# The first ten steps of a four-layer graph network in an order of their own, written out engine by engine

## What is computed

```
h = relu(layernorm(x))                      # ahead of every layer
layer 0: Wh = h @ W0; e = leaky(Wh@a1 + (Wh@a2).T); p = softmax(where(adj > .5, e, -9e15), axis=1)
         x = x + elu(p @ Wh)
layer 1: Ah = adj + I; d = rsqrt(rowsum(Ah)); x = x + relu((d*Ah*d) @ h @ W1 + bias)
layer 2: x = x + relu(adj @ h @ W2) * rowmask(h)
layer 3: x = x + relu([h, adj @ h / deg] @ W3.T)
```

## Time and profile before

| | us |
|---|---|
| median of 3 runs (2557.01 to 2562.32) | 2560.43 |
| the profiled execution: its time, and its span in the trace | 2557.61, 2555.8 |
| PE busy | 2482.3 (97% of the span) |
| DVE busy | 2021.0 (79%) |
| ACT busy | 1397.8 (55%) |
| POOL busy | 1224.1 (48%) |
| chain that ended last: PE's share | 95% |

### The profile page before, as it was taken

The page is one execution under the profiler, slowest core; times in us unless marked ns, Lnnn a source line. Parts: engine busy times, 40 slices in busy tenths (PEclk is TensorE's granted clock), DMA queues, the critical chain, the costliest instruction groups (busy, mean ns, idle before and its releaser), DMA issues.

```text
span 2555.8 us, 40394 instructions
## 1 busy us (share of the span) xinstructions
PE 2482.3 (97%) x13094; PEld 2135.8 (84%) x13094; DVE 2021.0 (79%) x4373; ACT 1397.8 (55%) x2571; POOL 1224.1 (48%) x1607
## 2 busy tenths in 40 slices
PE   2799999999999999999999999999999999999998
PEld 2688888888888888888888888888888888888887
DVE  6788878888888888788888888888788878878853
ACT  3565555555555555555556555555555555555542
POOL 2545545544544544544544545445445455455431
PEclk8899999999999999999999999999999999999999
DMA  4112222222222222221221222222222222222210
GB/s 144 44 42 57 55 66 54 57 67 52 59 67 51 60 66 51 60 67 49 62 66 50 62 59 56 63 58 57 61 59 57 60 61 56 60 61 56 49 34 25
DMA packets 355889, 149.40 MB, mean 58 GB/s; under 512 B 279520, under 2 KB 320096, under 8 KB 355680
## 3 DMA queue, kind: packets, MB, share of 16 engines
q1 hardware_dynamic: 355680, 146.82, 22.8%
HBM read 81.13 MB, written 33.62 MB: 45 GB/s over the span
## 4 chain that ended last, share of the span: by engine, by line
PE 95%; DVE 1%; issue 1%; POOL 1%; ACT 1%; SPq 0%; DMA 0%; POOLq 0%; ACTq 0%; DVEq 0%
PE O L340 46%; PE T L340 35%; PE X L340 13%; POOL h_lo L832 0%; SPq L287 0%; ACT h L466 0%; DMA act_out<-w_all 0%; POOL xs L797 0%; DVE ht_lo L684 0%; DVE p_lo L663 0%; DVE scores L590 0%; DVE w_lo L580 0%; DVE ln_stats L608 0%; POOL ln_scale L818 0%; DVE t_lo L669 0%
## 5 line engine op out<-in xcount | busy, mean ns | idle before, releaser
L832 POOL TENSOR_TENSOR h_lo<-h,h_hi 128x512 fp32r<-128x512 f32 x384 | 541.0, 1430 | 356.5 <-ACT h_hi L472 356.5
L466 ACT ACTIVATE h<-xs,ln_bias,ln_scale 128x512 f32<-128x512 f32 x512 | 395.7, 810 | 436.7 <-POOL ln_bias L826 436.7
L340 PE MATMUL O<-w_hi,t_hi 128*128 128x512 f32 x1536 | 597.9, 389 | 0.0
L340 PE MATMUL O<-w_lo,t_hi 128*128 128x512 f32 x1536 | 597.7, 389 | 0.0
L340 PE MATMUL O<-w_hi,t_lo 128*128 128x512 f32 x1536 | 597.7, 389 | 0.0
L669 DVE TENSOR_TENSOR t_lo<-T,t_hi 128x512 fp32r<-128x512 f32 x512 | 347.0, 688 | 251.7 <-ACT t_hi L478 251.5
L478 ACT CAST t_hi<-T 128x512 fp32r<-128x512 f32 x512 | 297.3, 582 | 409.1 <-PE T L340 409.1
L797 POOL TENSOR_TENSOR xs<-xs,act_out 128x512 f32<-128x512 f32 x128 | 164.7, 1310 | 584.1 <-ACT act_out L505 549.0
L608 DVE BATCH_NORM_STATS2 ln_stats<-xs 128x6 f32<-128x512 f32 x512 | 329.1, 680 | 23.7 <-POOL xs L803 16.9
L340 PEld LDWEIGHTS O<-w_hi,t_lo 128*128 128x128 f32 x1536 | 288.3, 188 | 59.9
L340 PEld LDWEIGHTS O<-w_hi,t_hi 128*128 128x128 f32 x1536 | 288.4, 188 | 55.3 <-DVE t_lo L669 0.5
(11 more groups left out here) (96 smaller groups left out, 5045.1 us busy)
## 6 DMA issues: line engine op xcount, KB each, us to landing
xs<-x SPq DMA_DIRECT2D x64, 512.0 KB, 5.2
out<-xs SPq DMA_DIRECT2D x64, 512.0 KB, 3.5
h<-act_out SPq DMA_DIRECT2D x976, 32.0 KB, 1.9
a_raw<-adj_t SPq DMA_DIRECT2D x64, 256.0 KB, 2.7
a_rows<-adj SPq DMA_DIRECT2D x64, 256.0 KB, 2.7
wh_rows<-wh_dram SPq DMA_DIRECT2D x61, 128.0 KB, 4.3
xs<-w_all SPq DMA_DIRECT2D x6, 512.0 KB, 7.2
act_out<-w_all SPq DMA_DIRECT2D x2, 512.0 KB, 6.6
```

The costliest lines, as they stand in the source:

```text
L340: last = nc.tensor.matmul(psum, s, m, start=(start and n == 0 and i == 0), stop=(stop and n == len(pairs) - 1 and i == 2))
L466: nc.scalar.activation(h[:, k.odd, m], xs[:, k.xb, m], ACT.Relu, bias=ln_bias[:, k.quad, m:m + 1], scale=ln_scale[:, k.quad, m:m + 1], acc ...
L832: nc.gpsimd.tensor_tensor(h_lo[:, k.odd, m], h[:, k.odd, m], h_hi[:, k.odd, m].bitcast(F32), ALU.subtract).then_inc(h_lo_ready, 1)
```

## The change

1. `Plan` holds a list of steps: HEAD for the first ten, then (4,0), (3,1), (2,2), (1,3), (5,0) and so on as before, with no empty number ahead of the end. Step 15 of before, (0,3), is number 9; (4,0) is 10; from there every step has its old number less 6.
2. ACT, DVE and POOL run a written-out list for everything ahead of slot 8, then their loops. PE keeps its loop, with `project` ahead of `gather` in the slots 0, 1, 5 and 8.
3. SP loads the first weight half ahead of x; x(1) to x(3) and a(1) to a(3) come earlier; x(4) and x(5) wait for weight halves. Tiles `dump` and `spare` are added: dump takes the unused results of the dots, spare stages the weight halves 5 and 8 and z half 9, in the place of xs[3] and xs[4].
4. `project_first` and the own term wait for ht_lo half by half, inside `h_times`.
5. SPREAD is 5. Waits that counted back 2 to 5 slots count to the last earlier step. POOL's first `low_part` waits for the weight vectors. The scratch for dynamic DMA is 4096 instead of 8192.

```diff
-SPREAD = 3
+SPREAD = 5
+HEAD = ((0, 0), (1, 0), (2, 0), (0, 1), (1, 1), (3, 0), (0, 2), (2, 1), (1, 2), (0, 3))
+FIRST, FILL = -5, 8
+PROJECT_FIRST = (0, 1, 5, 8)
...
+        tail = [(n - layer, layer) for n in range(LAYERS, graphs + LAYERS - 1) for layer in range(LAYERS)]
+        self.steps = [s if s[0] < graphs else None for s in list(HEAD) + tail]
...
-        stage = [act_out[:, 0], act_out[:, 1], z[:], xs[:, 5], xs[:, 4], xs[:, 3], z[:], xs[:, 5], xs[:, 4], xs[:, 3]]
+        stage = [act_out[:, 0], act_out[:, 1], z[:], xs[:, 5], xs[:, 4], spare[:], z[:], xs[:, 5], spare[:], z[:]]
...
-            load_x(0)
+            load_half(0)
             sp.dma_start(v_rows[:].rearrange("p v n -> p (v n)"),
...
-            load_half(0)
             load_half(1)
+            load_x(0)
             load_a(0)
             sp.dma_start(a_rows[:], tiles(adj, 0)).then_inc(rows_loaded, 16)
             load_x(1)
+            load_a(1)
+            load_x(2)
             load_half(2)
             load_half(3)
...
             def h_times(k, psum, n, w):
                 c = slice(n * P, n * P + P)
-                return product(psum, [(ht_hi[:, f, c], ht_lo[:, f, c], w_hi[:, w, f], w_lo[:, w, f]) for f in range(FT)])
+                for half in range(2):
+                    wait(pe, ht_lo_ready, k.part(L3, NT, half))
+                    last = product(psum, [(ht_hi[:, f, c], ht_lo[:, f, c], w_hi[:, w, f], w_lo[:, w, f])
+                                          for f in range(HALF * half, HALF * half + HALF)], start=half == 0, stop=half == 1)
+                return last
...
             for j in slots:
+                if j in PROJECT_FIRST:
+                    project_step(step(j))
                 if step(j + 2).layer == 0 and step(j + 2).g < SPREAD:
                     spread(step(j + 2))
...
+                gather_step(step(j + 1))
-                if step(j + 2).layer == 3 and not step(j + 2).carried:
+                if step(j + 2).layer == 3 and not step(j + 2).carried and j >= FILL:
                     transpose_h(step(j + 2))
```

DVE's written-out list, as far as the prediction follows it (`step(3)` is (0,1), `step(4)` is (1,1), `step(5)` is (3,0)); ACT's and POOL's are of the same kind:

```diff
+            vector_columns(0)
+            statistics(step(0))
+            vector_columns(1)
+            with_self(step(3))
+            add_mask(step(0))
+            vector_rows()
+            dots(step(0))
+            statistics(step(1))
+            split_weight(0)
+            split_weight(1)
+            mask_scores(step(0))
+            dots(step(1))
+            softmax_parts(step(0))
...
+            both(step(0))
+            statistics(step(2))
+            softmax_parts(step(1))
+            dots(step(2))
+            positive_part(step(0))
...
+            both(step(1))
+            statistics(step(3))
+            softmax_parts(step(2))
+            split_weight(2)
+            with_self(step(4))
+            positive_part(step(1))
+            both(step(2))
+            degrees(step(2))
+            split_weight(3)
+            both(step(3))
+            statistics(step(4))
+            statistics(step(5))
+            dots(step(5))
+            add_mask(step(5))
+            positive_part(step(2))
+            mask_scores(step(5))
+            both(step(4))
...
-            for j in slots:
+            for j in slots[FILL - FIRST:]:
```

ACT's, from where it meets DVE's `with_self(step(4))`:

```diff
+            activate(step(3))
+            high_part(step(3))
+            elu(step(1))
+            both(step(2))
+            with_self(step(4))
+            split_weight(3)
+            both(step(3))
+            activate(step(4))
+            high_part(step(4))
+            activate(step(5))
+            high_part(step(5))
```

More of the change, by code:

```diff
@@ L61, in count @@
     def count(self, k, layers):
-        return sum(min(max((k - self.position(0, n)) // LAYERS + 1, 0), self.graphs) for n in layers)
+        return sum(1 for s in self.steps[:max(k + 1, 0)] if s and s[1] in layers)
 class Step:
@@ L81, in done, with before @@
         return per * self.plan.count(self.k - back, layers)
+    def before(self, layer, layers, per=1):
+        return per * self.plan.count(self.plan.position(self.g, layer), layers)
     def part(self, layers, per, n, back=0):
@@ L218, in gnn_kernel @@
             sem("pool_added"), sem("out_ready"))
-        slots = range(-SPACING, plan.last + 2)
+        slots = range(FIRST, plan.last + 2)
         def step(k):
@@ L303, in _ @@
                     scores_in(step(j + 3))
[L304 to L310, removed]
+                if j in (1, 2):
+                    load_half(5 + j)
+                if j == 4:
+                    sp.wait_ge(w_lo_ready, 5)
+                    load_x(4)
+                if j in (5, 6):
+                    load_half(3 + j)
+                if j == 7:
+                    sp.wait_ge(w_lo_ready, 8)
+                    load_x(5)
                 old = step(j - 2)
@@ L480, in transposed @@
             def transposed(k):
-                wait(act, z_psum_ready, k.done(L3, NT, back=4))
+                wait(act, z_psum_ready, k.done(L3, NT, back=1))
                 if k.carried:
@@ L492, in own_term @@
             def own_term(k):
-                wait(act, out_ready, k.done(L3, back=4))
+                wait(act, out_ready, k.done(L3, back=1))
+                wait(act, w_lo_ready, 2 * WEIGHTS)
                 for n in range(NT):
@@ L498, in elu @@
             def elu(k):
-                wait(act, pool_added, k.done(L02, NT, back=2))
+                wait(act, pool_added, k.done(L02, NT, back=1))
                 for n in range(NT):
@@ L516, in exps @@
             def exps(k):
-                wait(act, neg_ready, k.done(L0))
+                act.wait_ge(neg_ready, k.done(L0))
                 for m in range(NT):
@@ L623, in dots @@
                         nc.vector.tensor_tensor_reduce(
-                            out=flat((scores, mask_add)[v][:]), in0=h[:, k.odd, m],
+                            out=dump[:, v], in0=h[:, k.odd, m],
                             in1=v_rows[:, v], scale=1.0, scalar=0.0, op0=ALU.mult, op1=ALU.add,
@@ L634, in mask_scores @@
             def mask_scores(k):
-                wait(dve, mask_ready, k.done(L0))
+                dve.wait_ge(mask_ready, k.done(L0))
                 if k.g < SPREAD:
@@ L695, in scaled_relu @@
                     dve.wait_ge(bias_in, 16)
-                wait(dve, deg_rsqrt_ready, k.done(L0, back=SPACING))
+                wait(dve, deg_rsqrt_ready, k.before(0, L0))
                 wait(dve, ht_moved, MOVES * plan.carried_count(k.k + 2))
@@ L744, in without_self, with both @@
                 nc.vector.tensor_tensor(diag, raw_diag, hi_diag, ALU.subtract).then_inc(a_lo_ready, 1)
+            def both(k):
+                gathered(k, 0)
+                gathered(k, 1)
             dve.wait_ge(ident_ready, 1)
-            for j in slots:
-                if j == -4:
-                    weight_vectors()
+            vector_columns(0)
+            statistics(step(0))
+            vector_columns(1)
+            with_self(step(3))
+            add_mask(step(0))
+            vector_rows()
@@ new lines, in _ @@
+            mask_scores(step(5))
+            both(step(4))
+            softmax_parts(step(5))
+            with_self(step(7))
+            split_weight(4)
+            scaled_relu(step(3))
+            degrees(step(5))
+            both(step(5))
+            without_self(step(6))
+            statistics(step(6))
+            statistics(step(7))
+            split_weight(5)
+            scaled_relu(step(4))
+            both(step(6))
+            without_self(step(8))
+            statistics(step(8))
@@ L750, in _ @@
+            split_weight(6)
+            positive_part(step(5))
+            both(step(7))
+            with_self(step(11))
+            split_weight(7)
+            both(step(8))
+            statistics(step(9))
+            statistics(step(10))
+            statistics(step(11))
+            dots(step(10))
+            add_mask(step(10))
+            transposed(step(9))
+            split_weight(8)
+            for j in slots[FILL - FIRST:]:
                 if step(j + 2).layer == 0:
@@ L819, in normalise @@
                 if k.layer == 1:
-                    wait(pool, deg_rsqrt_ready, k.done(L0, back=SPACING))
+                    wait(pool, deg_rsqrt_ready, k.before(0, L0))
                     wait(pool, rstd_ready, k.done(L1))
```

207 lines of the change are left out of this document (151 added, 56 removed).

## The result

On one chip (chip A below), nine executions each: before 2558.47 us (2557.01 to 2562.32), after 2551.09 us (2548.94 to 2553.54). The ratio is 0.9968 [0.9959, 0.9976]: 7.4 us less, where I had forecast 11.5 less and a range that holds 2551. The profiled execution of after took 2552.76 us with a span of 2551.0; it is 1.7 above its median, that of before 0.9 under its own, so the two traces differ by 4.8 us and not by 7.4.

A forecast was written before the change was run, and what follows sets the result against it. PE was taken to bound the kernel from 200 to 1000 us, leaving gains only at start and end: -9.6 - 1.9 = -11.5 us, from a median of 2560.4 to 2548.9, say 2549; range 2541 to 2558.

The forecast's parts named there:

- Idleness of the start: PE's idle time up to graph 2's own term: claimed to fall from 64.5 to 58.9 us.
- the walk: Hand simulation of the start, each engine taking its list in order; trusted to about 1 us.
- The 9.0 in front of the spread: PE's gap before the gather of (1,1): spread(3,0) stands ahead, waiting for dots of (3,0); longest new wait, 9.0 us.
- The 3.8 ahead of the gather of (0,1): PE's gap at the start, 3.8 us, while DVE stands 4.3 us in with_self(1,1) for ACT's copy.
- half clock 5.6 against 10.0 (two falls instead of four): Time PE loses at half clock in the start: 5.6 us after the change, 10.0 before.
- a rival at 0.13: Clock falls more often, behind the start's 3.2 and 3.8 us gaps: gain only 7.6, time 2552.8 us; chance 0.13.
- forecast start of -9.6: Start of the program, up to graph 2's own term: less idleness and half clock, two more spreads; -9.6 us.
- the yardstick: Start of PE's own term of graph 2, same work done in both orders: 235.40 before, about 225.8 forecast.
- so the middle is the same: Steps between start and end keep their parity and distance of five, so no change there: 0 us.
- The end: Last three ht_lo waits: PE starts after the first ht_lo half instead of the second; -1.9 us.
- Added waits at 0: The 448 added waits in h_times, in project_first and the own term, cost 0; other end 0.04 us each.
- The rival that the split waits cost 17.9 us: In h_times throughout, 448 waits at 0.04 us each: net +6.4 us, 2566.8, slower; chance 0.05.

The follow-up runs named there:

- both changes together: The changed kernel with PE's spreads and DVE's and ACT's start work reordered, plus 58 idle matmuls in PE's start gaps; 0.996 of before, 2555.2 us on chip C.

## Why the prediction was right or wrong

The number came near by luck; two of the steps behind it failed.

- **Idleness of the start: right.** 64.5 to 58.9 in the walk, 64.3 to 58.8 in the traces. The first gather began at 31.48, forecast 32.1. The 9.0 in front of the spread was 8.6, the 3.2 was 3.3, and the dots of (3,0) did alternate with h_lo, though from 78.5 to 84.6 and not from 72.5 to 78.9.
- **The 3.8 ahead of the gather of (0,1) was 5.67.** DVE stood 6.3 us for ACT's copy, not 4.3, and POOL's small ln_scale took 1.87 us instead of 0.2, behind three operations of DVE, back to back. In the walk I had let DVE and POOL take turns at the large operations only.
- **Failed: "half clock 5.6 against 10.0 (two falls instead of four)".** It was 13.7. The forecast's four slow places before are the slow first gather and three falls (the one at 84.8 is missing from my list of them); after has the first gather and four falls. The step that failed is my reading that only idleness of 4.3 us and more is followed by a fall: PEclk also fell behind the gaps of 3.31, 5.67 and 3.06 us, for which the walk had 3.2, 3.8 and 2.9. I had the first two as a rival at 0.13, with the argument that no shorter gap in the trace was passed at full clock; I should have seen that the same trace spoke no less for that rival than for my forecast. (It did have shorter cases: at its end PE passed 2.50 us of idleness at full clock.) It is 8.1 us of a forecast start of -9.6. The last 1.3 went with the two waits for t_lo at 193.85 and 232.74, where the walk had none (gaps behind 160 us were one of my signs of being wrong): the yardstick came at 235.80, 10 later than forecast. The first layer 3 began at 146.06, forecast 138 to 139.
- **Failed: "so the middle is the same".** I had concluded from PE busy for 800 of 800 us that no wait could be removed, and had read PE's waits alone. The wait sat at the weight loads, 58 times 0.2, and the change removed it: -5.5 in the trace. I priced the halves at the three waits of the end only.
- **The end: -1.9 was -1.2.** PE starts 0.14 behind the first half, where I had 0.04, and the first of these halves takes 0.70 instead of 0.59; the rest of the difference stays open. A fall of the clock at 2531, which I had not reckoned with, took 1.6 back.
- **Added waits at 0: right.** 24 matmuls still take 5.44 with three or four waits in them. The rival that the split waits cost 17.9 us has fallen.
- The total came near, 2551.1 against 2549, because two errors of opposite sign met: some 9.9 too much at the start, 5.5 too little in the middle. It also stood on a median of before from three executions, 2560.4; from the 2558.5 of nine the same forecast would give 2547.0. (The lower end, 2541, is 1 us under its own sum, 2560.4 - 14.3 - 4.) The mechanism that I gave for the gain isn't the one that made it.

## What to carry to other kernels

When an engine's matmul rows are gapless, read the waits of its weight loads and the length of one whole product as well: 0.2 us at a load, once per graph, was worth more than ten rearranged steps. When a start is rearranged, sum idleness and half clock apart, and count as slow what runs behind every gap of the length that the trace doesn't show passed at full clock. A written-out order should be tried with each instruction that only prepares a later step put behind the one that could go at once; that, on three engines, made 6 us here.

## What the runs showed of the hardware that I had not expected

PE's clock was at half behind gaps of 3.31 us and of 3.06 (rows at 45.65 and 117.58 above, PEclk 0.57 and 0.50 behind them). Before, the shortest idleness that I had seen ahead of a fall was 4.3 us. The length of the gap in front does not decide alone: PEclk fell behind 1.99 us ahead of the last project_first of after, and not behind 2.50 at the same place of before, nor behind the same 1.99 in the trace of both changes together. The rows of before and after:

```profile
2536.37 0.50 PE L340 MATMUL T<-w_hi,ht_hi 128*128 128x512 f32 x1 [2.50 <-DVE ht_lo L684]
```

```profile
2529.94 0.47 PE L358 MATMUL T<-w_hi,ht_hi 128*128 128x512 f32 x1 [1.99 <-DVE ht_lo L779]
```

The Trainium skill (TensorE: Matmul & The Clock Gate, "Why this matters for your kernels") wants idle gaps between bursts of matmuls short; these traces agree, for shorter gaps than I had allowed for.

A small operation of POOL can be shut out by DVE for long. After, POOL's timeline, and DVE's at that time:

```profile
54.56 1.87 POOL L987 TENSOR_TENSOR ln_scale<-ln_rstd,deg_rsqrt 128x2 f32<-128x2 f32 x1
```

```profile
54.03 0.88 DVE L758 SCALAR_TENSOR_TENSOR p_lo<-scores,s_rec,p_hi 128x256 fp32r<-128x256 f32 x2
54.82 1.22 DVE L673 TENSOR_TENSOR w_lo<-z,w_hi 128x1024 fp32r<-128x1024 f32 x1
55.96 0.42 DVE L827 TENSOR_TENSOR a_diag<-a_raw,ident 128x256 f32<-128x256 f32 x1
```

It begins while p_lo is made and ends at 56.43, just after the last of the three; the same operation took 0.20 before. The Trainium skill (SBUF — State Buffer, "SBUF: two separate sides") describes the shared port pair of the two engines as held for a whole instruction, with the other side blocked; the rows agree for each of DVE's operations. That POOL's waiting one also let the next two of DVE pass is only what these rows suggest.

A wait at a weight load shows as a longer matmul, with no idle time on PE: 0.23 us of waiting made the matmul 0.08 longer, a third of it. And the same kernel took 2558.5 us on chip A and some 2568 on B and C, 0.4% more, which is more than the change brings; only kernels run on the same chip can be compared.
